# Channel attention with turned weights, and linear attention with one product for values and gate

## The reference, cut to what matters

```python
# channel attention (layer 0): attention over the 256 channels of one sequence
q, k, v = x @ Wq, x @ Wk, x @ Wv                 # x is the layer-normed input, (128, 256)
w = softmax(q.T @ k / sqrt(8))                   # (256, 256)
y = (w @ v.T).T @ Wo ;  x = x + y

# linear attention (layer 1): 16 heads of 16, one chunk of 128 positions
q, k = rotate(silu(x @ Wq)), rotate(silu(x @ Wk)) ;  v = x @ Wv
o = ((q @ k.T) * decay) @ v                      # per head, causal decay
gate = x @ Wg1 @ Wg2                             # Wg1 (256, 16), Wg2 (16, 256)
u = o * sigmoid(gate) ; u = u * rsqrt(mean_head(u*u) + eps) * norm_weight
x = x + u @ Wo
```

## Time and profile before

| | us |
|---|---|
| median of 3 runs (lowest, highest) | 1319.75 (1319.05, 1320.85) |
| the profiled execution, its own time | 1320.28 |
| its span, first to last instruction | 1318.3 |
| PE busy, share of the span | 1182.8, 90% |
| DVE busy | 774.4, 59% |
| POOL busy | 603.9, 46% |
| ACT busy | 580.5, 44% |

### The profile page before, as it was taken

One profiled execution on the slowest core, in us unless ns is written; L12 is line 12 of the kernel. 1 busy time (PEld: TensorE's weight loads), 2 busy tenths in 40 slices (PEclk: granted clock), 3 DMA queues, 4 the chain that ended last, 5 costly groups with the idle time before them and its releaser, 6 DMA issues. The chain is left out here.

```text
span 1318.3 us, 24667 instructions
## 1 busy us (share of the span) xinstructions
PE 1182.8 (90%) x7421; PEld 831.5 (63%) x7422; DVE 774.4 (59%) x1930; ACT 580.5 (44%) x1504; POOL 603.9 (46%) x752
## 2 busy tenths in 40 slices
PE   7997889967989869978999999999999759999995
PEld 5774556544555534446888888888888536666663
DVE  4553688865887749955667767767666422222221
ACT  3432676643333300016656766666676323333331
POOL 2001465533655537636556666656665112232322
PEclk9998999988999979979999999999999869999998
DMA  7000000002998030041000000000002212222323
GB/s 259 0 0 12 14 18 12 13 1 81 187 206 170 1 154 12 0 188 72 5 13 13 13 15 15 20 12 12 12 17 77 85 43 42 47 44 44 47 41 88
DMA packets 46354, 69.41 MB, mean 53 GB/s; under 512 B 4736, under 2 KB 42672, under 8 KB 45232
## 3 DMA queue, kind: packets, MB, share of 16 engines
q1 hardware_dynamic: 37136, 52.95, 15.1%
q0 software_dynamic: 7152, 9.34, 4.4%
q10 hardware_dynamic: 2000, 6.29, 1.3%
HBM read 57.12 MB, written 32.58 MB: 68 GB/s over the span
## 5 line engine op out<-in xcount | busy, mean ns | idle before, releaser
L1742 PE MATMUL ga.pkq<-ga.xnT,g.early 128*128 128x128 f32 x1280 | 157.0, 276 | 1.0 <-ACT ga.halves L1660 1.0
L1742 PEld LDWEIGHTS ga.pkq<-ga.xnT,g.early 128*128 128x128 f32 x1280 | 151.6, 193 | 9.6 <-issue 8.2
L1522 POOL TENSOR_TENSOR ga.halves<-ga.halves,g.ga_sinT 128x512 f32<-128x512 f32 x80 | 103.3, 1291 | 51.6 <-ACT ga.halves L1660 51.6
L1786 PE MATMUL ga.turn_out<-g.early,ga.aT 128*128 128x256 f32 x512 | 118.3, 385 | 0.3 <-ACT ga.aT L1682 0.3
L1667 ACT ACTIVATE ga.e<-ga.psc,ga.negmax 128x128 f32<-128x128 f32 x256 | 90.6, 366 | 46.9 <-DVE ga.negmax L1588 45.9
L1530 POOL TENSOR_TENSOR ga.kqT<-ga.by_cos,ga.halves 128x512 f32<-128x512 f32 x80 | 102.6, 1283 | 16.5 <-issue 16.5
L1786 PEld LDWEIGHTS ga.turn_out<-g.early,ga.aT 128*128 128x128 f32 x512 | 95.9, 192 | 12.7 <-ACT ga.aT L1682 0.7
L1897 DVE TENSOR_TENSOR ex.hidden<-ex.silu,ex.p 128x512 f32<-128x512 f32 x39 | 26.8, 687 | 124.3 <-PE ex.p L1950 117.9
L1575 DVE TENSOR_TENSOR ga.by_cos<-ga.pkq,g.ga_cosT 128x512 f32<-128x512 f32 x80 | 55.3, 691 | 72.5 <-PE ga.pkq L1742 44.6
L1767 PE MATMUL ga.paT<-ga.pT,ga.v 128*128 128x512 f32 x128 | 68.4, 617 | 12.3 <-ACT ga.pT L1675 9.1
L1945 PE MATMUL ex.p<-g.spare,ex.xnT 128*128 x156 | 76.9, 616 | 1.1 <-ACT ex.xnT L1925 0.8
(11 more groups left out here) (290 smaller groups left out, 2630.2 us busy)
## 6 DMA issues: line engine op xcount, KB each, us to landing
mo_rows<-in_pad_rows SPq DMA_DIRECT2D x1, 18447.0 KB, 101.4
ex.row<-mo_rows SPq DMA_DIRECT2D x39, 129.0 KB, 2.1
g.spare<-in_mo_w SPq DMA_DIRECT2D x1, 4096.0 KB, 12.1
g.late<-in_mo_w SPq DMA_DIRECT2D x1, 4096.0 KB, 22.7
g.early<-in_mo_w SPq DMA_DIRECT2D x1, 4096.0 KB, 12.4
g.ctxT<-in_ctxR SPq DMA_DIRECT2D x1, 2048.0 KB, 11.9
xa.ctxT<-in_ctxT SPq DMA_DIRECT2D x16, 128.0 KB, 2.5
g.spare<-cv_rows SPq DMA_DIRECT2D x1, 2048.0 KB, 8.0
```

The lines of the kernel that those rows point to most:

```text
L1522: nc.gpsimd.tensor_tensor(by_sin[:, par, :].rearrange("p (h t) -> p h t", h=REP), halves[:, par, :].rearrange("p (h t) -> p h t", h=REP), ...
L1742: last = nc.tensor.matmul(pkq[:, par, j * P:(j + 1) * P], w[:, q, at * P:(at + 1) * P], xnT[:, s.par, q, :], start=(q == 0), stop=(q == C ...
L1786: last = nc.tensor.matmul(pout, aT[:, h // REP, (h % REP) * P:(h % REP + 1) * P], g.ga_wo[:, h, :], start=(h == 0), stop=(h == H - 1))
```

## The change

In channel attention the softmax weights are no longer multiplied into a scaled output matrix. PE turns `w` (four transposes into a new PSUM tile `pwT`), DVE copies the result to `wT` (128x512), and one step later PE multiplies `wT` with `vT` into `pmix` (now 128x256: eight records of 128 columns). ACT copies that to `mixed` in two instructions of 128x128, each scaled with the reciprocal sums, and PE multiplies `mixed` with the unscaled output matrix, later in the same step. DVE's copy of `vT` moves ahead of its statistics; the two multiplications for `wo` are gone.

In linear attention Wg1 @ Wg2 is computed once, ahead of the steps, and put beside Wv in one tile `la_wvg` of 256 rows by 512 columns; Wg1 is now loaded transposed. Values and gate come from one product of 512 columns into `pvx` where values took four records of 256. The products L1064 and L1085 and ACT's copy L1007 are gone. The turning of the normed input (PE) and its copy (ACT) move from the head of step s to the middle of step s-1. `k` is turned into `pvx` instead of `turn2`, and ACT's copy of `kT` no longer waits for `qT`. The output of item s-2 goes to the free half of `turn`. In `allocate` the tiles that follow in the `early` buffer shift accordingly, and `la_vd` moves.

The diff, without `allocate`, declarations of tiles and semaphores, the names of the loads and the host's layouts:

```diff
--- before.py
+++ after.py
@@ -341,16 +341,18 @@
         dve.wait_ge(w_ready, upto(b))
-        nc.vector.reciprocal(rowsum[:, b.par, :], rowsum[:, b.par, :])
-        dve.drain()
-        if b.base is None and b.n == 0:
-            dve.wait_ge(g.ca_o_loaded, 16)
+        nc.vector.reciprocal(rowsum[:, b.par, :], rowsum[:, b.par, :]).then_inc(sum_ready, 1)
+    if s.on:
+        dve.wait_ge(vT_done, upto(s))
+        if s.past(2):
+            dve.wait_ge(mix_done, upto(s, back=2))
+        nc.vector.tensor_copy(vT[:, s.par, :, :], pv[:, 0:D]).then_inc(vT_ready, 1)
+    b = s.back(1)
+    if b.on:
+        dve.wait_ge(w_turned, upto(b))
         if b.past(2):
             dve.wait_ge(mix_done, upto(b, back=2))
-        for c in range(C):
-            last = nc.vector.tensor_scalar(wo[:, b.par, c, :], g.ca_wo[:, c, :], rowsum[:, b.par, c:c + 1],
-                                           None, ALU.mult)
-        last.then_inc(wo_ready, 1)
+        nc.vector.tensor_copy(wT[:, b.par, :, :], pwT[:]).then_inc(wT_ready, 1)
     b = s.back(-2)
@@ -359,11 +361,6 @@
         layer_norm_stats(nc, m, g.x[:, b.i, :], b.par, var_ready)
-    if s.on:
-        dve.wait_ge(vT_done, upto(s))
-        if s.past(2):
-            dve.wait_ge(out_done, upto(s, back=2))
-        nc.vector.tensor_copy(vT[:, s.par, :, :], pv[:, 0:D]).then_inc(vT_ready, 1)
 steps(dve, step, 2, 2)
@@ -374,11 +371,22 @@
         nc.scalar.activation(xnT[:, s.par, :, :], turn[:, 0:D], ACT.Copy).then_inc(xnT_ready, 1)
+    b = s.back(2)
+    if b.on:
+        act.wait_ge(mix_done, upto(b))
+        act.wait_ge(sum_ready, upto(b))
+        if b.past(2):
+            act.wait_ge(out_done, upto(b, back=2))
+        for c in range(C):
+            last = nc.scalar.activation(mixed[:, b.par, c, :], pmix[:, c * P:(c + 1) * P], ACT.Copy,
+                                        scale=rowsum[:, b.par, c:c + 1])
+        last.then_inc(mix_ready, 1)
     b = s.back(1)
...
         if b.past(2):
-            act.wait_ge(mix_done, upto(b, back=2))
+            act.wait_ge(w_turned, upto(b, back=2))
+            act.wait_ge(mix_ready, upto(b, back=2))
         for c in range(C):
@@ -388,11 +396,6 @@
         nc.scalar.activation(qk[:, s.par, :], pqk[:], ACT.Copy).then_inc(qk_ready, 1)
-    if b.on:
-        act.wait_ge(mix_done, upto(b))
-        if b.past(2):
-            act.wait_ge(out_done, upto(b, back=2))
-        nc.scalar.activation(mix[:, b.par, :, :], pmix[:], ACT.Copy).then_inc(mix_ready, 1)
 steps(act, step, 0, 2)
@@ -418,14 +421,15 @@
     if b.on:
-        pe.wait_ge(mix_ready, upto(b))
+        pe.wait_ge(wT_ready, upto(b))
         pe.wait_ge(vT_ready, upto(b))
         if b.past(1):
-            pe.wait_ge(x_added, upto(b, back=1))
+            pe.wait_ge(mix_ready, upto(b, back=1))
         for c in range(C):
-            last = nc.tensor.matmul(pout[:, 0:D], vT[:, b.par, c, :], mix[:, b.par, c, :],
-                                    start=(c == 0), stop=(c == C - 1))
-        last.then_inc(out_done, 1)
+            for f in range(C):
+                last = nc.tensor.matmul(pmix[:, c * P:(c + 1) * P], wT[:, b.par, f, c * P:(c + 1) * P],
+                                        vT[:, b.par, f, :], start=(f == 0), stop=(f == C - 1))
+        last.then_inc(mix_done, 1)
     if s.on:
@@ -435,6 +439,18 @@
         last.then_inc(qk_done, 1)
+    b = s.back(2)
+    if b.on:
+        pe.wait_ge(mix_ready, upto(b))
+        if b.base is None and b.n == 0:
+            pe.wait_ge(g.ca_o_loaded, 16)
+        if b.past(1):
+            pe.wait_ge(x_added, upto(b, back=1))
+        for c in range(C):
+            last = nc.tensor.matmul(pout[:, 0:D], mixed[:, b.par, c, :], g.ca_wo[:, c, :],
+                                    start=(c == 0), stop=(c == C - 1))
+        last.then_inc(out_done, 1)
+    if s.on:
         if s.base is None and s.n == 0:
@@ -446,14 +462,13 @@
     if b.on:
-        pe.wait_ge(wo_ready, upto(b))
+        pe.wait_ge(w_ready, upto(b))
         if b.past(1):
-            pe.wait_ge(mix_ready, upto(b, back=1))
+            pe.wait_ge(wT_ready, upto(b, back=1))
         for f in range(C):
             for c in range(C):
-                last = nc.tensor.matmul(pmix[:, f, :], w[:, b.par, c, f * P:(f + 1) * P], wo[:, b.par, c, :],
-                                        start=(c == 0), stop=(c == C - 1))
-        last.then_inc(mix_done, 1)
+                last = nc.tensor.transpose(pwT[:, f, c * P:(c + 1) * P], w[:, b.par, c, f * P:(f + 1) * P], g.ident[:])
+        last.then_inc(w_turned, 1)
 steps(pe, step, 0, 2)
@@ -980,31 +994,24 @@
         def _(act):
+act.wait_ge(wg_done, 1)
+nc.scalar.activation(g.la_wvg[:, :, D:2 * D], pvx[:].rearrange("p (c n) -> p c n", c=C), ACT.Copy).then_inc(wg_ready, 1)
+
 def step(s):
-    a, b, c = s.back(2), s.back(1), s.back(3)
-    if s.on:
-        act.wait_ge(turned, upto(s))
-        if s.past(2):
-            act.wait_ge(v_done, upto(s, back=2))
-        nc.scalar.activation(xnT[:, s.par, :, :], turn[:, 0:D], ACT.Copy).then_inc(xnT_ready, 1)
+    a, b, c, n1 = s.back(2), s.back(1), s.back(3), s.back(-1)
     if a.on:
...
         act.wait_ge(qk_turned, upto(b))
-        act.wait_ge(qT_ready, upto(b))
         if b.past(2):
             act.wait_ge(scores_done, upto(b, back=2))
-        nc.scalar.activation(kT[:, b.par, :, :], turn2[:, 1, :, :], ACT.Copy).then_inc(kT_ready, 1)
+        nc.scalar.activation(kT[:, b.par, :, :], pvx[:, 0:D], ACT.Copy).then_inc(kT_ready, 1)
     if s.on:
...
         nc.scalar.activation(qk[:], pqk[:], ACT.Silu).then_inc(silu_ready, 1)
-        act.wait_ge(g1_done, upto(s))
-        if s.past(1):
-            act.wait_ge(gate_done, upto(s, back=1))
-        nc.scalar.activation(g1T[:], turn[0:16, D:D + P], ACT.Copy).then_inc(g1_ready, 1)
         act.wait_ge(v_done, upto(s))
@@ -1012,8 +1019,12 @@
             act.wait_ge(u_ready, upto(s, back=2))
-        act.wait_ge(gate_done, upto(s))
-        nc.scalar.activation(gate[:, s.par, :], turn[:, 0:D], ACT.Tanh, scale=0.5).then_inc(gate_ready, 1)
+        nc.scalar.activation(gate[:, s.par, :], pgate, ACT.Tanh, scale=0.5).then_inc(gate_ready, 1)
+    if n1.on:
+        act.wait_ge(turned, upto(n1))
+        if n1.past(2):
+            act.wait_ge(v_done, upto(n1, back=2))
+        nc.scalar.activation(xnT[:, n1.par, :, :], turn[:, 0:D], ACT.Copy).then_inc(xnT_ready, 1)
     if a.on:
@@ -1027,31 +1038,30 @@
         nc.scalar.activation(g.cv_qT[:, c.par, :, bass.ds(c.i * (P // 2) - c.par * (P // 2), P)], px2.rearrange("p (c t) -> p c t", c=C), ACT.Copy).then_inc(qT2_ready, 1)
-steps(act, step, 0, 3)
+steps(act, step, 1, 3)
 
...
 pe.wait_ge(filled, 1)
+for k in range(C):
+    last = nc.tensor.matmul(pvx[:, k * D:(k + 1) * D], g.la_wg1T[:, k * P:(k + 1) * P], g.la_wg2, start=True, stop=True)
+last.then_inc(wg_done, 1)
 
 def step(s):
-    a, b, c = s.back(2), s.back(1), s.back(3)
-    if s.on:
-        pe.wait_ge(xn_ready, upto(s))
-        if s.past(1):
-            pe.wait_ge(gate_ready, upto(s, back=1))
-        for k in range(C):
-            last = nc.tensor.transpose(turn[:, k * P:(k + 1) * P], xn[:, s.par, k * P:(k + 1) * P], g.ident[:])
-        last.then_inc(turned, 1)
+    a, b, c, n1 = s.back(2), s.back(1), s.back(3), s.back(-1)
     if b.on:
         pe.wait_ge(qk_ready, upto(b))
+        pe.wait_ge(v_ready, upto(b))
+        pe.wait_ge(gate_ready, upto(b))
         if b.past(1):
...
             pe.wait_ge(qT2_ready, upto(s, back=4))
-        for t in range(2):
-            for k in range(C):
-                last = nc.tensor.transpose(turn2[:, t, k, :], qkr[:, b.par, t * D + k * P:t * D + (k + 1) * P], g.ident[:])
+        for k in range(C):
+            nc.tensor.transpose(turn2[:, 0, k, :], qkr[:, b.par, k * P:(k + 1) * P], g.ident[:])
+        for k in range(C):
+            last = nc.tensor.transpose(pvx[:, k * P:(k + 1) * P], qkr[:, b.par, D + k * P:D + (k + 1) * P], g.ident[:])
         last.then_inc(qk_turned, 1)
@@ -1060,10 +1070,6 @@
         last.then_inc(qk_done, 1)
-        for k in range(C):
-            last = nc.tensor.matmul(turn[0:16, D:D + P], g.la_wg1[:, k, :], xnT[:, s.par, k, :],
-                                    start=(k == 0), stop=(k == C - 1))
-        last.then_inc(g1_done, 1)
     if b.on:
@@ -1076,13 +1082,11 @@
     if s.on:
-        if s.past(3):
-            pe.wait_ge(x_added, upto(s, back=3))
+        if s.base is None and s.n == 0:
+            pe.wait_ge(wg_ready, 1)
         for k in range(C):
-            last = nc.tensor.matmul(pv, xnT[:, s.par, k, :], g.la_wv[:, k, :], start=(k == 0), stop=(k == C - 1))
+            last = nc.tensor.matmul(pvx[:], xnT[:, s.par, k, :], g.la_wvg[:, k, :], start=(k == 0), stop=(k == C - 1))
         last.then_inc(v_done, 1)
-        pe.wait_ge(g1_ready, upto(s))
-        nc.tensor.matmul(turn[:, 0:D], g1T[:], g.la_wg2, start=True, stop=True).then_inc(gate_done, 1)
     if c.on:
@@ -1090,6 +1094,13 @@
         last.then_inc(turned2, 1)
+    if n1.on:
```

(30 more changed lines are left out.)

17 lines of the change are left out of this document (8 added, 9 removed).

## The result

The changed kernel took 1304.21 us (median of 5 runs, 1303.52 to 1305.45) against 1319.75 us (5 runs, 1319.05 to 1324.10): a ratio of 0.9877, 95% interval 0.9862 to 0.9893. The profiled execution took 1305.45 us, 2.0 over its span of 1303.5.

The account below looks back on a forecast made before the run. PE's work was taken to bound channel attention and one closing chain of 10.01 us a step linear attention. Gains of 6.2 and 8.0 us, 14.2 together, took 1319.75 to 1305.5 us; forecast 1303 to 1308, range 1302 to 1311.

Parts of the forecast that it names:

- PE's step in channel attention: Channel attention: PE's work falls from 6.28 to 5.86 us a step; 5.95 taken because of DVE's loop; thirteen steps give 4.3 us.
- rival A: Channel attention: DVE becomes the bound, steps stay at 6.28 us, only 1.9 us gained there, 1309.9 in all; chance 0.12.
- The step before them: Channel attention, item 1 to item 2, without output or weight product yet: 5.00 us for 6.92, a gain of 1.9 us.
- ACT's two scaled copies: Channel attention: 0.73 us for both, hidden under `pqk` (1.72) between `pmix` and the output product, so they cost nothing.
- The narrow product: Linear attention: the product with Wg1 leaves the closing chain, 0.55 us a step, fourteen steps, 7.7 us.
- the 512-column product hides behind the scores: Linear attention: it and the transposes end 3.29 us after the scores' start, `un` is ready at 3.83, so hidden.
- The moved transposes at nothing: Linear attention: turning the input a step ahead gains nothing, since `pqk` waits for `u`; at most 0.21 us.
- The opening of linear attention: Ahead of its steps: added work costs 0 to 0.4 us, an earlier clock rise gains 0 to 0.9; 0.3 net gain taken.
- No other stage is touched: Whole kernel: each other stage starts when the one before ends, so no term was given to any of them.
- B: Linear attention: POOL's norm, with 0.13 us of slack, becomes the bound; 0.3 later loses 3.8 us, 1309.3; chance 0.10.
- C: Channel attention: less multiplying and more transposing lowers the granted clock; slower, 1329 with a quarter of the steps; chance 0.03.
- D: Both stages: the narrow product was hidden and PE's channel-attention work not the bound; time stays within 0.2%; chance 0.03.

Follow-up runs that it names:

- the fill at the opening: Changed kernel plus three 512-column products of no use on PE at the opening of cross-attention, where PE otherwise stands idle: 1303.13 us, ratio 0.9871 to the kernel before.
- a move of four lines: Kernel before, with only linear attention's product with Wg1 moved on PE from ahead of the scores to behind them: 1314.80 us, ratio 0.9949.

## Why the prediction was right

Forecast 1305.5, measured 1304.21: -14.2 against -15.5. That the sum came so near is in part luck. By the stages of the two traces channel attention gave 0.6 us more than forecast, linear attention 1.2 less, and 1.2 came from stages that had no term; another 0.7 lies between the medians and the traces. The mechanism of both halves is what the experiments show. The single terms:

**PE's step in channel attention.** Summed 5.86, measured 5.89 (four transposes took 0.44, not 0.42); 5.95 had been taken, for DVE's loop. Latency from output product to addition was 1.19, inside the 1.03 to 1.28; `wT` took 0.69, the value taken. DVE's loop came out at 5.83 to 5.87, just under PE, so rival A did not come, by 0.02 to 0.06 us. Thirteen steps gave 5.55 us for the 4.3 forecast: 13 x (6.28 - 5.905) = 4.9 by the steps, and 0.7 since of the startup disturbance, which had been left in, 0.36 us remained of 1.04 (77.13 is 13 x 5.905 and 0.36 over). All other traces with the old channel attention had only 0.24 of it, and 81.88 us from item 2 to 15; against those the gain is 4.75, and 0.8 of the 5.55 are chance.

**The step before them.** 5.02 for the 5.00 forecast, against 6.92. On the other side item 0 to 1 took 6.04 for 5.41, since the clock rose later in that run (`pv` of item 0 took 1.55 us for 1.05; the distance is 5.4 to 6.5 over all traces of both versions). The stage's tail cost nothing, as said: 12.92 us from the last `pqk` to the next stage, 12.91 before. ACT's two scaled copies (0.62 for both, 0.73 forecast) are hidden.

**The narrow product.** 0.55 a step was forecast, 0.51 measured: 7.1 us instead of 7.7. Unrolled steps gained 0.54; in the loop it was 0.37 to 0.43 in each second step, for `u` stands 0.58 behind the addition there, with 0.16 us of issue at the loop's turn. This is the term whose size was off. That the 512-column product hides behind the scores held: the last transposes behind it end 3.33 us after the scores' start (380.46 + 0.22 - 377.35; 3.29 forecast), and `un` is ready 3.83 after it, as forecast.

**The moved transposes at nothing.** Right for this change, but for half a reason. Put back at the head they cost 0.6 a step, since the tile that they are turned into now carries the output. "Worth nothing" was read from the chain of the kernel before, where that tile was free.

**The opening of linear attention.** A net gain of 0.3 by the clock was forecast; it did not come. The product of the gate matrices starts at 290.96, and `pqk` of item 0 still takes 3.78 us, as in the earlier trace rows:

```profile
290.96 2.04 PE L1048 MATMUL la.pvx<-g.early 16*128 16x256 f32 x4 [1.62 <-DVE g.early L924]
...
294.10 3.78 PE L1071 MATMUL la.pqk<-g.early,la.xnT 128*128 128x512 f32 x4 [0.47 <-ACT la.xnT L1027]
```

Linear attention gave 6.8 us for 8.0: 0.6 less by the steps, 0.3 by the opening, and 0.3 longer ends.

**"No other stage is touched".** That step failed. The stages are separate in their data and their order, but not in the clock: the fill at the opening showed that the level there follows PE's idle time around the turn, part of which lies at the end of the stage ahead. Cross-attention brought 2.3 us, and 1.1 were lost in the last two stages, where single traces scatter as much (grouped attention 486.7 to 490.0 us); without both the sum of what was predicted (13.6 by the traces, 14.2 forecast) would have stood for the whole.

**The rivals.** A missed by 0.02 to 0.06 us a step, B by the 0.13 that had been read the earlier trace rows. B's price was wrong in the prediction: a norm 0.3 us later, less 0.13 of slack, is 0.17 a step and 2.4 us, not 0.27 and 3.8; the norm 0.33 later cost 0.20 and 2.8. So was C's count: PE does 1.73 - 0.89 = 0.84 us less multiplication a step, not 1.31. C did not come: with six transposes a step channel attention is granted 1.00. The rule of the Trainium skill that it rested on ("TensorE: Matmul & The Clock Gate", Part 4: PE-mode transpose) did not decide anything here. D is out by the two halves run alone.

## What to carry to other kernels

Find the closing chain of a step and ask of each link whether it could stand elsewhere in its engine's order before asking for less work: here a move of four lines equalled, in its stage, a change that rebuilt the products. Where two loops close within a tenth of a microsecond of each other, as PE's and DVE's in channel attention or norm and decay product in linear attention, the next gain needs both. Moving an instruction is free only for the tiles as they are; if the same change gives its tile a second use, cost the move again.

## What the runs showed of the hardware

**The clock at the turn of stages** moved the time of untouched code by 2 to 4 us: cross-attention, the same instructions in every trace, took 180.8 to 185.4 us without a filling. On one chip 23 runs of the kernel before ranged from 1317.3 to 1323.8 us; that this spread is the clock's too is likely by the traces, in which nothing else differs by as much, but it wasn't tested. A difference of 2 us between single traces of one stage says nothing until it is divided into the parts where the clock is low.

**DVE beside POOL's memset.** The startup disturbance of channel attention is a DVE operation on 128x2 values, 0.17 us otherwise, that ends when POOL's filling of a tile ends. In the kernel before, timeline:

```profile
19.11 1.22 DVE L329 TENSOR_SCALAR ca.negmax<-ca.negmax 128x2 f32<-128x2 f32 x1
...
19.29 1.01 POOL L310 MEMSET g.early<- 128x1088 f32 x1
```

In the kernel after, the same line beside another fill:

```profile
18.17 2.02 DVE L329 TENSOR_SCALAR ca.negmax<-ca.negmax 128x2 f32<-128x2 f32 x1
...
18.32 1.85 POOL L209 MEMSET g.spare<- 128x2112 f32 x1
```

What decides it is not shown. In the second trace of the kernel before the same two rows start as far apart, 0.18 us (19.90 and 20.08), and DVE's takes 0.26: it ends at 20.16, with the filling before, which ends at 20.14. In all eight traces of the new channel attention the row takes 2.02. The Trainium skill ("SBUF — State Buffer", Who interferes with whom) says that a DVE operation of this kind, when it runs in a mode that uses two ports, and a GpSimd one take a shared pair of ports in turn, each for its whole length, the one issued first going first. The ends of these rows agree (20.33 beside 20.30, 20.19 beside 20.17); the order does not show in them, since both DVE rows start ahead of the filling with which they end. No run took the fill away.
